# Masked attention with its mask, normalisation and projection steps in other slots, early key stores, and mixture layers computed in rows

## The chip, the cores and the metric

The kernel runs on one core of one Trainium2 chip. The metric is the device time of one execution in microseconds (us). The engines are named as the profile names them: PE (TensorE matmuls), PEld (its weight loads), DVE (VectorE), ACT (ScalarE), POOL (GpSimd) and SP (the sync engine, which here issues all loads and stores).

## The reference

A stack of four layer pairs works on x, 32 sequences of 56 tokens with 128 features, against a context of 32 x 1500 x 128. Every pair adds `tanh(g) * attention(layernorm(x), context)` and then `tanh(g) * ffn(layernorm(x))`. The change touches the first attention, and the third and the fourth feed-forward layer:

```python
# attention of pair 0: 16 heads of 8 features, with nan/inf clamps on q, k, v and the bias
logits = jnp.einsum('bhqd,bhkd->bhqk', q, k) * scale + bias
logits = jnp.where(mask == 0, -10000.0, logits)
probs = jax.nn.softmax(logits, axis=-1)
out = jnp.einsum('bhqk,bhkd->bhqd', probs, v)          # then @ W_o.T + b_o
# ffn of pair 2: 8 experts of one 128x128 matrix, top 2 of a softmax router, weights normalised
# ffn of pair 3: 8 experts with a bias each, top 1, weighted by its probability
out_all = jnp.einsum('th,ehd->ted', xt, expert_w) + expert_b[None, :, :]
e_out = jnp.take_along_axis(out_all, idx[:, None, None], axis=1)[:, 0, :]
y = gate[:, None] * e_out
```

## The kernel before

The program is a chain of blocks, and all engines meet between two of them: a block that loads x, then for each layer a `norm` block and the layer's own. In the trace the masked attention (`masked_attention`) covers about 0 to 1610 us, the other three attentions most of the rest; the two mixture layers in question lie at 4943 to 5027 us and 6161 to 6250 us.

**Masked attention.** It goes through the 32 sequences ("batches"). The 16 heads of a batch are handled in 8 pairs, one to a slot, p = 0 to 7; a pair has 2 x 56 = 112 query rows and 1500 keys. In slot p PE computes the pair's scores in two halves (`score(n, p, 0)` and `score(n, p, 1)`), transposes the logits of the pair of two slots ago in three portions (`turn`), and does one portion of other work. DVE turns each half's scores into logits with the bias and their maximum (`shifted(n, p, 0)` and `(n, p, 1)`), and `negate` closes the slot. There are two score buffers: `score(p, h)` waits until `shifted(p - 1, h)` is done. ACT subtracts the maximum, takes the exponential and copies PE's small results out.

Beside this, keys and values of batch n + 2 are prepared in batch n, in three portions each. PE computes the raw keys in slots 0 to 2 (`keys`) and the raw values in slots 3 to 5 (`values`); ACT copies keys out, DVE values (`keep_values`, slots 3 to 5). POOL guards each portion (`guard`: it clamps, 3 instructions), DVE takes the cleaned portion (`take`, slots 2 to 7: keys in 2 to 4, values in 5 to 7) and marks what is finite (`finite`). Keys are split in three bf16 parts (DVE's first, then POOL's `split`), stored to a scratch in DRAM (`store_keys`) and read back in packed form (`load_keys`) when the ring of packed keys has room. There are two buffers of key parts, so `take` of portion 2 in slot 4 waits for the store of portion 0. POOL's order in a batch is guard 0, guard 1, split 0, guard 2, split 1, guard 3, split 2, `blocks` (the queries of the next batch), guard 4, guard 5.

The mask of batch n + 1 arrives in three portions through one small buffer (`load_mask`), and DVE turns each into bf16 (`mark`, slots 0, 2 and 4). A load waits for the mark before it. The transposed mask (`load_mask_t`, one tile of 125 x 672, marked by `mark_t` in slot 5) serves two products in slots 0 and 1 of the next batch (`weigh_masked`), and its load waits until they are done. The end of a batch falls into the next one: `add_masked` in slot 5, PE's `sums` in slot 6, DVE's `normalise` (4 instructions, the first is the reciprocal) in slot 6, PE's output projection `out` at the end of slot 7, and ACT's `finish` at the head of slot 0 after it. SP issues everything in one written order, and each issue can wait on a semaphore, which holds back all behind it.

**Mixture layers.** `route` computes router logits and, in a chain of small DVE instructions, the combine weights `ffn_cw` (16 tiles of 112 tokens x 8 experts). PE then spreads each expert's weights over 128 partitions, 128 small matmuls, whose results ACT and DVE copy out. `experts`, a block of its own, multiplies the transposed input by an expert's weights on DVE and adds 8 x 4 products of 448 columns in PSUM. The result is feature by token, so the next `norm` block transposes it back and adds it to x.

## Time and profile before

| | |
|---|---|
| runs | 6254.1, 6254.86, 6259.9 us; median 6254.86 us |
| profiled execution | 6263.05 us, of which the span of its instructions is 6261.3 us |
| busy in the span | PE 86%, PEld 62%, DVE 71%, ACT 51%, POOL 29% |
| mean granted clock of PE | 0.927 |
| masked attention, 250 to 1500 us | PE busy 1116.20, DVE 1050.01, POOL 850.76, ACT 815.09 us of 1250; clock 0.92 |

A granted clock of 1.00 is 2.4 GHz, 0.50 is 1.2 GHz. Times in the timeline count from the span's start. An instruction's length can overlap the start of the next on its engine by about 0.1 us. "x2" merges instructions of one kind.

### The profile page before, as it was taken

To read this page: it belongs to the slowest core of one execution; us is meant where nothing else is said; L and a number is where in the kernel's file an instruction comes from. 1 tells how busy PE (TensorE), PEld (TensorE's weight loads), DVE (VectorE), ACT (ScalarE), POOL (GpSimd) and SP (SyncE) were. 2 spreads that over 40 slices of the span, in tenths; PEclk is the share of its full clock that TensorE was granted. 3 is DMA by queue.
4 is the path that set the end of the run, shared out by engine and by line. 5 is a ranking of instruction groups with operands and counts; after the bars stand their busy time and mean duration, and the time that the engine had idled before them with its cause. 6 is when DMAs were issued, how large, how long until landed. Compare 5 with 4: busy or idle time off the path is not lost. (4 is left out here: it accounts for less than half of the span.)

```text
span 6261.3 us, 134129 instructions
## 1 busy us (share of the span) xinstructions
PE 5379.5 (86%) x51967; PEld 3896.8 (62%) x51967; DVE 4432.3 (71%) x9168; ACT 3198.4 (51%) x5984; POOL 1820.4 (29%) x1426
## 2 busy tenths in 40 slices
PE   2888889899569999989749999999999759999997
PEld 1777777777258888877724444444444437888786
DVE  6888888887257777763458777777777437777774
ACT  0666666666236666652224444444444216666662
POOL 4767676763022222211101111111111012222220
PEclk6899999999679999989969999999999769999998
DMA  4555555553167777742010000000000048888880
GB/s 110 120 125 122 124 123 121 124 119 82 37 123 139 139 140 139 140 87 103 26 33 15 15 15 15 18 17 15 15 15 5 7 94 159 159 161 160 158 151 10
DMA packets 368548, 545.59 MB, mean 87 GB/s; under 512 B 115780, under 2 KB 248006, under 8 KB 367606
## 3 DMA queue, kind: packets, MB, share of 16 engines
q1 hardware_dynamic: 365894, 533.81, 41.7%
q8 instruction: 384, 6.29, 0.5%
q0 software_dynamic: 2048, 3.67, 0.2%
q14 instruction: 222, 1.82, 0.1%
HBM read 413.45 MB, written 123.90 MB: 86 GB/s over the span
## 5 line engine op out<-in xcount | busy, mean ns | idle before, releaser
L652 DVE CUSTOM_DVE_ANT_0 attn_logits<-attn_scores,attn_shift 112x750 f32<-112x750 f32 x1024 | 945.0, 933 | 441.3 <-PE attn_scores L456 441.3
L568 ACT ACTIVATE attn_probs_t<-attn_pt 125x448 f32<-125x448 f32 x1536 | 831.0, 542 | 579.3 <-PE attn_pt L471 559.0
L471 PEld LDWEIGHTS attn_pt<-ident,attn_logits 112*125 112x125 f32 x6144 | 850.9, 188 | 178.6 <-issue 92.5
L471 PE MATMUL attn_pt<-ident,attn_logits 112*125 112x112 f32 x6144 | 920.1, 273 | 25.5 <-ACT attn_logits L559 24.4
L2264 PE MATMUL attn2k_pk<-attn_wk,attn2k_cn_t 128*125 128x512 f32 x1536 | 738.7, 603 | 53.3 <-ACT attn2k_cn_t L2335 36.8
L2275 PE MATMUL attn2k_pg<-attn2k_kn,attn2k_cn 125*128 125x512 f32 x1536 | 725.0, 594 | 6.1 <-ACT attn2k_gram L2343 3.9
L2430 DVE TENSOR_REDUCE attn2k_ss<-attn2k_sq 125x16 f32<-125x1024 f32 x384 | 466.9, 1216 | 256.9 <-ACT attn2k_sq L2372 256.9
L385 POOL CAST attn_k_parts<-xn_t 128x500 bf16<-128x500 f32 x192 | 199.5, 1039 | 1421.6 <-DVE xn_t L622 1421.6
L1159 ACT ACTIVATE attn_probs_t<-attn_pt 125x448 f32<-125x448 f32 x768 | 414.9, 541 | 309.9 <-PE attn_pt L1047 308.2
L2372 ACT ACTIVATE attn2k_sq<-attn2k_pk 125x1024 f32<-125x1024 f32 x384 | 391.9, 1021 | 324.9 <-PE attn2k_pk L2264 324.8
L2264 PEld LDWEIGHTS attn2k_pk<-attn_wk,attn2k_cn_t 128*125 128x125 f32 x1536 | 273.1, 187 | 416.9 <-issue 321.0
L456 PE MATMUL attn_scores<-attn_k_packed,attn_q_blocks 96*112 96x375 bf16 x2048 | 514.4, 333 | 15.9 <-POOL attn_q_blocks L375 13.2
L1035 PE MATMUL attn_scores<-attn_k_packed,attn_q_blocks 96*112 96x375 bf16 x1024 | 357.4, 349 | 148.0 <-DVE attn_tops L1328 148.0
L2442 DVE TENSOR_TENSOR attn2k_kn<-attn2k_pk,attn2k_rn 125x1024 f32<-125x1024 f32 x384 | 470.0, 1224 | 13.3
L2275 PEld LDWEIGHTS attn2k_pg<-attn2k_kn,attn2k_cn 125*128 125x128 f32 x1536 | 264.1, 192 | 299.7 <-issue 287.9
L1328 DVE CUSTOM_DVE_ANT_0 attn_logits<-attn_scores,attn_bias,attn_floor 112x750 f32<-112x750 f32 x342 | 337.8, 988 | 101.6 <-PE attn_scores L1037 99.2
L1148 ACT ACTIVATE attn_logits<-attn_logits,attn_neg_top 112x750 f32<-112x750 f32 x342 | 313.0, 916 | 112.5 <-DVE attn_neg_top L1336 110.4
L559 ACT ACTIVATE attn_logits<-attn_logits,attn_neg_top 112x750 f32<-112x750 f32 x384 | 351.4, 915 | 4.1 <-DVE attn_neg_top L660 0.9
L2246 POOL COPY attn2k_q_now<-attn_q_t 128x448 f32 (+1 forms) x32 | 17.8, 557 | 1153.7 <-PE attn2k_pz L2296 1153.7
L412 PE MATMUL attn_side<-attn_ctx_t,attn_wk 128*128 128x500 f32 x384 | 221.5, 660 | 149.1 <-DVE xn_t L622 82.7
L484 PE MATMUL attn_po<-attn_probs_t,attn_v 125*32 125x112 f32 x12288 | 347.8, 261 | 1.5 <-ACT attn_probs_t L568 1.3
L1037 PE MATMUL attn_scores<-attn_masked,attn_pusher 112*112 112x375 bf16 x1024 | 344.8, 337 | 0.0
(364 smaller groups left out, 10562.6 us busy)
## 6 DMA issues: line engine op xcount, KB each, us to landing
attn_k_packed<-k_scratch SPq DMA_DIRECT2D x384, 375.0 KB, 6.4
attn_k_packed<-k_scratch SPq DMA_DIRECT2D x384, 187.5 KB, 3.9
k_scratch<-attn_k_parts SPq DMA_DIRECT2D x64, 1125.0 KB, 7.4
attn_ctx_t<-in_ctx_t SPq DMA_DIRECT2D x64, 750.0 KB, 7.3
k_scratch<-attn_k_parts SPq DMA_DIRECT2D x96, 375.0 KB, 4.4
attn_ctx_t<-in_ctx_t SPq DMA_DIRECT2D x96, 250.0 KB, 5.2
attn2k_ctx<-in_ctx SPq DMA_DIRECT2D x32, 750.0 KB
attn_mask_in<-in_mask SPq DMA_DIRECT2D x192, 109.4 KB
```

Source lines behind the costliest of these rows:

```text
L456: last = pe.matmul(scores[h][0:PAIR, b, 0:QTR], q_blocks[:, n % 2, p, :, :].rearrange("p a s -> p (a s)"), k_packed[:, n % 2, p, h * HALF ...
L471: last = pe.transpose(pt[(3 * at + t) % 2][0:KC, (c % 4) * PAIR:(c % 4 + 1) * PAIR], logits[:, at % 3, c * KC:(c + 1) * KC], g.ident[0:PAI ...
L559: act.activation(at, at, ACT.Identity, bias=neg_top[:, n % 2, p:p + 1]).then_inc(act_lowered, 1)
L568: act.activation(probs_t[0:KC, p // 4, 4 * t:4 * t + 4, (p % 4) * PAIR:(p % 4 + 1) * PAIR], pt[(3 * at + t) % 2][0:KC, 0:QUAD].rearrange(" ...
L652: dve.tensor_tensor_reduce(out=logits[:, at % 3, cols].rearrange("p (b k) -> p b k", b=2), in0=scores[h][0:PAIR, :, 0:QTR], in1=shift[:, n ...
L1035: pe.matmul(scores[h][0:PAIR, b, 0:QTR], q_blocks[:, n % 2, p, :, :].rearrange("p a s -> p (a s)"), k_packed[:, at % KEY_RING, cols], star ...
L1159: act.activation(probs_t[0:KC, at % PV_RING, 4 * t:4 * t + 4, :], pt[(3 * at + t) % 2][0:KC, 0:QUAD].rearrange("p (c q) -> p c q", c=4), A ...
L2264: last = pe.matmul(pk[c % 2][0:KC, b, :], cn_t[:, c % 2, :], wk[:, b * HW:(b + 1) * HW], start=True, stop=True)
L2275: last = pe.matmul(pg[:, b, :], cn[:, j, c, :], kn[:, c % 2, b * HW:(b + 1) * HW], start=(c == 0), stop=(c == CH - 1))
L2372: act.activation(sq[:, c % 2, :].rearrange("p (a b) -> p a b", a=2), pk[c % 2][0:KC, :, :], ACT.Square).then_inc(sq_ready, 1)
L2430: dve.tensor_reduce(ss[:, c % 2, :], sq[:, c % 2, :].rearrange("p (h d) -> p h d", h=H2), AX.X, ALU.add).then_inc(ss_ready, 1)
L2442: dve.tensor_tensor(kn[:, c % 2, :].rearrange("p (h d) -> p h d", h=H2), pk[c % 2][0:KC, :, :].rearrange("p a (h d) -> p (a h) d", h=8), r ...
```

## The change

It has four parts.

1. In the masked attention DVE's marks of the mask move: portions 1 and 2 of batch n + 1 to slots 1 and 2, portion 0 of batch n + 2 to the end of slot 7, and `mark_t` to slot 0 of the batch after. `normalise` moves from slot 6 to the end of slot 7, and the projection `out` from the end of slot 7 to slot 0, between the two score halves; ACT's `finish` goes behind the first exponential of slot 0.
2. SP's order changes with it: `store_keys` of portions 0 and 1 come ahead of the loads of the second half of the packed keys, and the loads of mask portions 1 and 0 move.
3. `mixture` replaces `route` and `experts` for the two layers. For each tile of 112 tokens PE computes all 8 experts' outputs (2 matmuls of 512 columns). For 11 tiles DVE multiplies them by the combine weights and sums over experts, for 5 tiles ACT scales and POOL adds. The sum is added to x in the block itself, so no expert-wise spread, no separate block and no transposition back remain. Layer 3 adds its bias by transposed weights, quarter by quarter.
4. The `norm` blocks after these layers get no gate, and the last one issues only the store of x.

```diff
                 for n in range(B):
                     if n + 1 < B:
+                        load_mask(n + 1, 1)
                         load_keys(n + 1, 0, (0, 1))
-                        load_mask(n + 1, 1)
                         load_keys(n + 1, 0, (2, 3))
                     load_mask_t(n)
                     if n + 1 < B:
...
-                    for i in range(3):
-                        if n + 1 < B:
-                            load_keys(n + 1, 1, (2 * i, 2 * i + 1))
-                        if n + 2 < B:
-                            store_keys(n + 2, i)
-                        if n + 3 < B:
+                    if n + 2 < B:
+                        store_keys(n + 2, 0)
+                        load_mask(n + 2, 0)
+                        store_keys(n + 2, 1)
+                    if n + 1 < B:
+                        load_keys(n + 1, 1, (0, 1, 2))
+                    if n + 2 < B:
+                        store_keys(n + 2, 2)
+                    if n + 1 < B:
+                        load_keys(n + 1, 1, (3, 4, 5))
+                    if n + 3 < B:
+                        for i in range(3):
                             load_ctx(n + 3, i)
                     if n + 2 < B:
-                        load_mask(n + 2, 0)
                         load_queries(n + 2)
...
                         if some:
                             turn(*prior, 0)
+                        if p == 0 and n > 1:
+                            out(n - 2)
                         score(n, p, 1)
...
-                        if p == 7 and n > 0:
-                            out(n - 1)
+                out(B - 2)
...
-                        if p == 0 and n > 1:
-                            finish(n - 2)
                         for t in range(3):
                             if prior[0] >= 0:
                                 exp(*prior, t)
+                            if p == 0 and t == 0 and n > 1:
+                                finish(n - 2)
...
-                        if p in (0, 2, 4) and n + 1 < B:
-                            mark(n + 1, p // 2)
-                        if p == 5:
-                            mark_t(n)
+                        if n + 1 < B and (p in (1, 2) or p == n == 0):
+                            mark(n + 1, p)
+                        if p == 0 and n > 0:
+                            mark_t(n - 1)
                         shifted(n, p, 1)
...
-                        if p == 6 and n > 0:
-                            normalise(n - 1)
                         if p == 7 and n + 1 < B:
                             floors(n + 1)
                         negate(n, p)
+                        if p == 7 and n + 2 < B:
+                            mark(n + 2, 0)
+                        if p == 7 and n > 0:
+                            normalise(n - 1)
+                mark_t(B - 1)
```

The core of the new `mixture`, behind a router chain that is the one of before (the output of an expert has 128 columns, `py` is a ring of 3 tiles of 2 PSUM banks):

```python
ACT_TILES = tuple(t for t in range(TILES) if t % 3 == 2)
DVE_TILES = tuple(t for t in range(TILES) if t % 3 != 2)
# PE, after the router's matmuls
for t in range(TILES):
    if t >= 3:
        if t - 3 in ACT_TILES:
            pe.wait_ge(parts_ready, ACT_TILES.index(t - 3) + 1)
        else:
            pe.wait_ge(scaled_ready, DVE_TILES.index(t - 3) + 1)
    for c in range(2):
        last = pe.matmul(py[t % 3][0:PAIR, c, :], g.xn_t[:, t * PAIR:(t + 1) * PAIR],
                         we[:, 4 * c:4 * c + 4, :].rearrange("p e d -> p (e d)"), start=True, stop=True)
    last.then_inc(y_ready, 1)
if b_experts is not None:
    for q in range(NQ):
        wait(pe, x_steps, 2 * q)
...
# DVE, once cw is there
for i, t in enumerate(DVE_TILES):
    dve.wait_ge(y_ready, t + 1)
    wait(dve, summed, i - 1)
    dve.tensor_tensor(scaled[:, i % 2, :, :], values(t),
                      cw[:, t, :].unsqueeze(2).broadcast_to((PAIR, E, D)), ALU.mult).then_inc(scaled_ready, 1)
    dve.wait_ge(scaled_ready, i + 1)
    dve.tensor_reduce(total[:, t, :], scaled[:, i % 2, :, :].rearrange("p e d -> p d e"), AX.X,
                      ALU.add).then_inc(summed, 1)
```

The order of the instructions shows what stands where. On SP, in the middle of a batch, this stood before, from the transposed mask's load on (`out_t` is the transposed mask, `mask_in` a mask portion, `k_parts` to `k_scratch` a key store, `k_packed` a load of packed keys):

```order
L821 DMA attn0_out_t<-in_mask0_t 125x672
L817 DMA attn0_mask_in<-in_mask0 56x500 x2
L843 DMA attn0_k_packed<-k_scratch 16x4x1500 x2
L880 DMA y_scratch<-y_t 128x56
L843 DMA attn0_k_packed<-k_scratch 16x4x1500 x2
L832 DMA k_scratch<-attn0_k_parts 128x3x500
L812 DMA attn0_ctx_t<-in_ctx_t 128x500
```

and this stands there now:

```order
L822 DMA attn0_out_t<-in_mask0_t 125x672
L818 DMA attn0_mask_in<-in_mask0 56x500 x2
L844 DMA attn0_k_packed<-k_scratch 16x4x1500 x2
L881 DMA y_scratch<-y_t 128x56
L833 DMA k_scratch<-attn0_k_parts 128x3x500
L818 DMA attn0_mask_in<-in_mask0 56x500 x2
L833 DMA k_scratch<-attn0_k_parts 128x3x500
```

The first store of keys no longer stands behind a load of packed keys. The mask portion right behind the transposed mask is portion 2 in both, but its mark now stands in slot 2 and no longer in slot 4.

On DVE, at the end of slot 7 and in slot 0 (L1328 and L1335 are `shifted`, the row that writes only `tops` belongs to it), before:

```order
L1328 ISA x_sb,attn0_tops<-attn0_scores1,attn0_bias,attn0_floor 112x750
L1328 ISA attn0_tops 112x1
L1316 TENSOR_SCALAR attn0_floor<-attn0_counted 112x1
L1318 TENSOR_SCALAR attn0_floor<-attn0_floor 112x1
L1336 TENSOR_SCALAR attn0_neg_top<-attn0_tops 112x1
L1328 ISA attn0_logits0,attn0_tops<-attn0_scores0,attn0_bias,attn0_floor 112x750
L1328 ISA attn0_tops 112x1
L1258 TENSOR_SCALAR attn0_masked<-attn0_mask_in 112x500
```

and now:

```order
L1335 ISA x_sb,attn0_tops<-attn0_scores1,attn0_bias,attn0_floor 112x750
L1335 ISA attn0_tops 112x1
L1323 TENSOR_SCALAR attn0_floor<-attn0_counted 112x1
L1325 TENSOR_SCALAR attn0_floor<-attn0_floor 112x1
L1343 TENSOR_SCALAR attn0_neg_top<-attn0_tops 112x1
L1265 TENSOR_SCALAR attn0_masked<-attn0_mask_in 112x500
L1363 RECIPROCAL xn_t<-attn0_side 128x224
L1365 TENSOR_TENSOR xn_t<-attn0_mixed,xn_t 128x224
L1367 TENSOR_TENSOR attn0_mixed<-xn_t 128x224
L1369 COPY_PREDICATED xn_t<-attn0_mixed,attn0_zero 128x224
L1335 ISA attn0_logits0,attn0_tops<-attn0_scores0,attn0_bias,attn0_floor 112x750
```

A mark and the four instructions of `normalise` now stand between the end of slot 7 and the first logits of slot 0.

On PE, from the last product of slot 7 to the second score half of slot 0 (L1020 and L1026 are the projection), before:

```order
L1060 MATMUL attn0_po<-attn0_probs_t,attn0_v 32x112 x24
L1020 MATMUL attn0_side<-xn_t,attn0_wo 128x56 x4
L1035 MATMUL attn0_scores0<-attn0_k_packed,attn0_q_blocks 112x375
L1037 MATMUL attn0_scores0<-attn0_masked,attn0_pusher 112x375
L1035 MATMUL attn0_scores0<-attn0_k_packed,attn0_q_blocks 112x375
L1037 MATMUL attn0_scores0<-attn0_masked,attn0_pusher 112x375
L1047 MATMUL attn0_pt0<-ident,attn0_logits1 125x112 x4
L1035 MATMUL attn0_scores1<-attn0_k_packed,attn0_q_blocks 112x375
```

and now:

```order
L1066 MATMUL attn0_po<-attn0_probs_t,attn0_v 32x112 x24
L1041 MATMUL attn0_scores0<-attn0_k_packed,attn0_q_blocks 112x375
L1043 MATMUL attn0_scores0<-attn0_masked,attn0_pusher 112x375
L1041 MATMUL attn0_scores0<-attn0_k_packed,attn0_q_blocks 112x375
L1043 MATMUL attn0_scores0<-attn0_masked,attn0_pusher 112x375
L1053 MATMUL attn0_pt0<-ident,attn0_logits1 125x112 x4
L1026 MATMUL attn0_side<-xn_t,attn0_wo 128x56 x4
L1041 MATMUL attn0_scores1<-attn0_k_packed,attn0_q_blocks 112x375
```

The projection, which waits for `normalise`, stands ahead of the second score half of slot 0.

## Rows read from the trace of the kernel before

**Rows 1.** Waits, 250 to 1500 us: total us, times, longest us.

```profile
DVE attn_k_parts L1286 <- DMA k_scratch<-attn_k_parts: 46.8, 28, 2.1
```

**Rows 2.** Timeline of PE: start us, length us, instruction, [idle before].

```profile
807.25 0.56 PE L1035 MATMUL attn_scores<-attn_k_packed,attn_q_blocks 96*112 96x375 bf16 x1 [4.12 <-DVE attn_tops L1328]
...
812.83 0.37 PE L1035 MATMUL attn_scores<-attn_k_packed,attn_q_blocks 96*112 96x375 bf16 x1
...
818.33 0.32 PE L1035 MATMUL attn_scores<-attn_k_packed,attn_q_blocks 96*112 96x375 bf16 x1
...
821.22 1.10 PE L1020 MATMUL attn_side<-xn_t,attn_wo 128*128 128x56 f32 x8
...
823.22 0.32 PE L1035 MATMUL attn_scores<-attn_k_packed,attn_q_blocks 96*112 96x375 bf16 x1
...
831.85 0.37 PE L1035 MATMUL attn_scores<-attn_k_packed,attn_q_blocks 96*112 96x375 bf16 x1
...
851.46 0.56 PE L1035 MATMUL attn_scores<-attn_k_packed,attn_q_blocks 96*112 96x375 bf16 x1 [3.84 <-DVE attn_tops L1328]
```

**Rows 3.** Timeline of DVE, the same stretch.

```profile
836.71 0.82 DVE L1258 TENSOR_SCALAR attn_masked<-attn_mask_in 112x500 bf16<-112x500 int32 x1
...
843.83 0.68 DVE L1296 TENSOR_TENSOR y_t<-attn_side,attn_bv 125x512 f32<-125x512 f32 x1
...
861.36 1.54 DVE L1356 RECIPROCAL xn_t<-attn_side 128x224 f32<-128x224 f32 x1
...
864.15 0.20 DVE L1336 TENSOR_SCALAR attn_neg_top<-attn_tops 112x1 f32<-112x1 f32 x1
...
865.19 0.78 DVE L1303 COPY_PREDICATED attn_v<-attn_good,y_t 125x512 f32<-125x512 int32 x1
...
867.29 1.00 DVE L1328 CUSTOM_DVE_ANT_0 x_sb<-attn_scores,attn_bias,attn_floor 112x750 f32<-112x750 f32 x1
```

**Rows 4.** Timeline of POOL, the same stretch.

```profile
844.67 0.62 POOL L934 TENSOR_SCALAR y_t<-y_t 125x512 f32<-125x512 f32 x1
...
849.49 0.73 POOL L944 CAST attn_k_parts<-attn_clean_late 128x500 bf16<-128x500 f32 x1 [1.06 <-DVE attn_clean_late L1288]
...
860.33 1.25 POOL L937 TENSOR_TENSOR attn_v<-attn_v,y_t 125x512 f32<-125x512 f32 x1
```

**Rows 5.** Timeline of SP, its DMA issues, the same stretch.

```profile
831.98 0.28 SPq L821 DMA_DIRECT2D attn_out_t<-in_mask_t  x1
837.56 0.76 SPq L817 DMA_DIRECT2D attn_mask_in<-in_mask  x2
```

**Rows 6.** Windows; last three columns: clock, DMA share, GB per s.

```profile
834.00:837.80 3.80, 3.80 (x64) 2.96 (x63) 3.73 (x6) 2.82 (x5) 2.58 (x4) 1.00 0.20 80
839.70:841.00 1.30, 1.30 (x13) 1.21 (x12) 1.23 (x3) 1.19 (x2) 1.30 (x1) 1.00 1.10 180
```

**Rows 7.** Timeline, all engines, the two mixture layers.

```profile
4961.23 0.29 DVE L1680 TENSOR_TENSOR ffn_cw<-route_hot 112x128 f32<-112x128 f32 x1
...
5032.64 3.18 DVE L197 BATCH_NORM_STATS2 norm_stats<-x_sb 112x6 f32<-112x128 f32 x16
...
6174.96 0.29 DVE L1659 TENSOR_TENSOR ffn_cw<-route_hot,route_m 112x128 f32<-112x128 f32 x1
...
6207.65 0.53 ACT L1627 ACTIVATE ffn_cw_t<-route_pb 8x448 f32<-8x448 f32 x1 [0.73 <-PE route_pb L1611]
...
6251.91 3.12 DVE L183 SCALAR_TENSOR_TENSOR x_sb<-last_py,gates,x_sb 112x512 f32<-112x512 f32 x4 [8.00 <-PE last_py L158]
6255.06 0.34 SPq L230 DMA_DIRECT2D out<-x_sb  x1
```

**Rows 8.** The page's costliest groups: xcount, busy us, mean ns, idle us.

```profile
L2264 PE MATMUL attn2k_pk<-attn_wk,attn2k_cn_t 128*125 128x512 f32 x1536 | 738.7, 603 | 53.3 <-ACT attn2k_cn_t L2335 36.8
...
L2430 DVE TENSOR_REDUCE attn2k_ss<-attn2k_sq 125x16 f32<-125x1024 f32 x384 | 466.9, 1216 | 256.9 <-ACT attn2k_sq L2372 256.9
...
L2442 DVE TENSOR_TENSOR attn2k_kn<-attn2k_pk,attn2k_rn 125x1024 f32<-125x1024 f32 x384 | 470.0, 1224 | 13.3
```

More of the change, by code:

```diff
@@ L1613, in _ @@
                         last.then_inc(turned, 1)
+                        pe.wait_ge(cw_t_ready, q + 1)
+                        for t in range(4 * q, 4 * q + 4):
+                            last = pe.matmul(pb[0:PAIR, (t % 4) * D:(t % 4 + 1) * D], cw_t[:, t * PAIR:(t + 1) * PAIR],
+                                             be[:], start=True, stop=True)
+                        last.then_inc(bias_ready, 1)
             @block.scalar
@@ L1618, in _ @@
                 act.activation(p[:], p[:], ACT.Exp).then_inc(exp_ready, 1)
-                for i in range(0, E * NQ, 2):
-                    e, q = divmod(i, NQ)
-                    act.wait_ge(spread, i + 1)
-                    act.activation(cwb[:, e, q * QUAD:(q + 1) * QUAD], pb[i % 4][:, 0:QUAD],
-                                   ACT.Copy).then_inc(act_used, 1)
-                if cw_t is not None:
+                act.wait_ge(cw_ready, 1)
+                for i, t in enumerate(ACT_TILES):
+                    act.wait_ge(y_ready, t + 1)
+                    wait(act, halved, i - 1)
+                    for e in range(E):
+                        last = act.activation(parts[:, i % 2, e, :], values(t)[:, e, :], ACT.Copy, scale=cw[:, t, e:e + 1])
+                    last.then_inc(parts_ready, 1)
+                if b_experts is not None:
                     for q in range(NQ):
                         act.wait_ge(turned, q + 1)
-                        act.activation(cw_t[:, q * QUAD:(q + 1) * QUAD], pb[q][0:E, 0:QUAD],
-                                       ACT.Copy).then_inc(act_used, 1)
+                        act.activation(cw_t[:, q * QUAD:(q + 1) * QUAD], pb[0:E, 0:QUAD], ACT.Copy).then_inc(cw_t_ready, 1)
+            @block.gpsimd
+            def _(pool):
+                for i, t in enumerate(ACT_TILES):
+                    at = i % 2
+                    pool.wait_ge(parts_ready, i + 1)
+                    pool.tensor_tensor(halves[:, at, :, :], parts[:, at, 0:4, :], parts[:, at, 4:8, :], ALU.add).then_inc(halved, 1)
+                    pool.wait_ge(halved, i + 1)
+                    pool.tensor_tensor(halves[:, at, 0:2, :], halves[:, at, 0:2, :], halves[:, at, 2:4, :],
+                                       ALU.add).then_inc(added, 1)
+                    pool.wait_ge(added, 2 * i + 1)
+                    pool.tensor_tensor(total[:, t, :], halves[:, at, 0, :], halves[:, at, 1, :], ALU.add).then_inc(added, 1)
             @block.vector
@@ L1730, in ffn2 @@
[L1730 to L1745 removed]
+                dve.wait_ge(cw_ready, 1)
@@ new lines, in _ @@
+                dve.wait_ge(summed, len(DVE_TILES))
+                for q in range(NQ):
+                    rows = g.x[:, 4 * q:4 * q + 4, :].rearrange("p t d -> p (t d)")
+                    dve.wait_ge(added, 2 * sum(t < 4 * q + 4 for t in ACT_TILES))
+                    if b_experts is not None:
+                        dve.wait_ge(bias_ready, q + 1)
+                        dve.scalar_tensor_tensor(rows, pb[0:PAIR, :], g.gates[:, gate:gate + 1], rows,
+                                                 ALU.mult, ALU.add).then_inc(x_steps, 1)
+                        dve.wait_ge(x_steps, 2 * q + 1)
+                    dve.scalar_tensor_tensor(rows, total[:, 4 * q:4 * q + 4, :].rearrange("p t d -> p (t d)"),
+                                             g.gates[:, gate:gate + 1], rows, ALU.mult, ALU.add).then_inc(x_steps, 1)
@@ L2606, in program @@
                 mask=a["mask3"]), "add"),
-            lambda: ffn3(nc, g, a),
+            lambda: mixture(nc, g, "ffn3", a, a["router3"], a["router3_b"], "top1", a["experts3"], 7, a["experts3_b"]),
         ]
```

143 lines of the change are left out of this document (44 added, 99 removed).

## The prediction, made before the changed kernel ran

> **What bounds the kernel now.** I read the timeline of one batch of the masked attention first, engine by engine, because the change touches every one of the 30 batches that still prepare keys (n = 0 to 29), then the chain of waits for how often a wait recurs, then the timeline of the mixture layers. One batch takes 44.2 us: the second score half of slot 5 starts at 807.25 and, a batch later, at 851.46 [rows 2]. It is the only place where PE waits long, 4.12 and 3.84 us, and it waits for DVE's logits of slot 4. DVE itself had stood for the DMA that stores key portion 0; such waits sum to 46.8 us in 28 batches, 1.7 us each [rows 1]. After the wait PE runs at half clock: the score matmul at 807.25 takes 0.56 us, the same one at 823.22 0.32 us [rows 2].
>
> So the batch is a ring. From the wait on PE works without a pause to slot 2 (812.83 is the head of slot 6, 823.22 the second score half of slot 0, 831.85 the head of slot 2), and from there DVE, loaded with `take`, sets the pace to the end of slot 4. The slow stretch is on it: slot 5's work took 5.6 us (807.25 to 812.83); in the other slots such work runs at twice the speed, and I put the loss at 2.3 us.
>
> **The mixture layers.** Removed is all from `ffn_cw` to x. In layer 2 that is 4961.52 to 5032.64 (the first instruction of the next norm on x), 71.1 us; in layer 3 6175.25 to 6255.06, 79.8 us [rows 7]. What replaces it goes by DVE. An eight-expert tile is 1024 elements wide; a product and a reduction of that width cost 1.224 and 1.216 us [rows 8], with handover 2.5 us, and 11 tiles 27.5 us. PE needs at most 0.96 us per matmul of 512 columns (738.7 us over 768 of them, two records each) [rows 8], so 1.9 us per tile, 5.8 per three tiles against DVE's 5.0 for its two of three. But it is three tiles ahead when the weights arrive, and those rows include a slow clock and waits; I take 28.5 us in layer 2, where it has idled before, 27.5 in layer 3. ACT's and POOL's five tiles lie beside. Then four additions, 3.12 us [rows 7], and 1.1 us to the next block: 32.7 us, a saving of 38.4. In layer 3 the bias makes each quarter a chain of transposes, a copy of 0.53 us [rows 7], products and two additions of 0.78 each; the first hides behind DVE's tiles. I put the first at 1.6 and the other three at 4.0 each (below 2.1, the copy and additions alone; above 6): 27.5 + 1.6 + 12 + 1.1 = 42.2, a saving of 37.6. Together 76 us. The bound on the poor side is the reduction: its input here is strided, no row shows that, and at half rate 11 x 1.2 x 2 = 27 us would be lost. I take no loss, since the product and the reduction, which read in different patterns, cost the same.
>
> **The masked attention: what goes.** The key store no longer stands behind a load of packed keys that waits for slot 4, and is issued as POOL's first split ends, some 5 us earlier; the 1.7 us go. So does one mark of 0.8 us from slot 4 [rows 3], the transposed mask's from slot 5, and `normalise`, 861.36 to 864.15, 2.8 us [rows 3], from slot 6. DVE then reaches the value portions sooner. What is late next is POOL.
>
> **What binds then.** POOL is continuous from guard 3 at 844.67 to the end of guard 5 at 861.58, save 1.06 us of waiting for DVE [rows 4]: 15.85 us of work, none of it changed. Guard 3 begins when DVE has copied value portion 0 (843.83 + 0.68 = 844.51 [rows 3]), and DVE's slot 7 cannot go past `take` of portion 2 before guard 5 ends. Before, that `take` stood at 865.19, 3.6 us later than needed. DVE's own work between these two points falls from 20.7 us (844.44 to 865.19) to 20.7 - 1.6 - 0.8 - 0.4 - 2.8 = 15.1, so POOL is the later one by about 0.8 us.
>
> Behind that `take`: 865.19 to 867.29, 2.1 us, led to the logits of slot 0 [rows 3]; now a mark (0.4 us where POOL rests, by half of the 0.82 beside it) and `normalise` stand there too: 5.3 us. PE's projection waits for it, and the second score half of slot 0 stands behind the projection: 0.1 + 0.9 us. From there to slot 2 is unchanged, 823.22 to 831.85, 8.6 us [rows 2]. PE idles ahead of the projection. From slot 7's second score half to that point PE has 823.22 - 818.33 - 0.9 = 4.0 us of work [rows 2], DVE from the same instant at least 0.9 + 0.9 + 0.5 + 0.4 + 2.8 = 5.5 us, and POOL's delay adds to it: 2 to 3 us of idling, in slots where nothing hides it.
>
> **A new wait in slot 2.** Mask portion 2 is now marked in slot 2, due at 836.71 [rows 3]. Its load stands on SP behind the transposed mask, which waits until slot 1's masked products end: issued at 831.98 [rows 5], its 328 KB go at 80 GB/s and a low DMA share until 837.8 [rows 6]. Before, the portion was issued at 837.56, for slot 4, and nobody waited. Now it is issued at once, but moves behind the big load: 219 KB at the 180 GB/s of the next window [rows 6] are 1.2 us, to 839.0. If the portion uses other DMA engines it is there at 835.6 and there is no wait. I take 838.6, a wait of 1.9 us (bounds 0 and 2.3).
>
> The Trainium skill, page "DMA: Bandwidth & Descriptors", section "Why a DMA increments its semaphore by 16 and not by 1", says that a load from SP runs on the largest number of engines up to 16 that divides its outer dimension, the lowest-numbered ones: 5 for this mask of 125 rows, 14 for a portion of 56 rows, which share those 5; and descriptors of an engine are taken in ring order ("Queues, rings and completion order"). The DMA share of 0.20 agrees roughly (5 of 16 would be 0.31). By the rule the wait is there in every batch; without it, 29 x 1.9 = 55 us would fall out of the sum.
>
> **The sum of a batch.** From the head of slot 2: 844.51 - 831.85 = 12.7; mask wait 1.9; POOL 0.15 + 15.85 + 0.1; DVE 5.3; projection 1.0; PE to slot 2 8.6. That is 45.6 us, against 44.2. The old 2.3 us of slow clock are no longer on the ring, but three waits of 2 to 3 us (slots 3, 5, 0) replace the one of 4. Whether a wait of that length lowers the clock no row shows, since PE's next longest wait in a batch of before is far shorter than 3.84. So the cost lies between 0 and 2.3 us; I take 0.7, nearer to nothing, since the waits are shorter and only the part that falls in slots 0 and 1 counts. The batch becomes 46.3, +2.1 us, in 29 periods +61 us. Prologue and tail change by less than 2 us.
>
> In all 6263 - 76 + 61 = 6248 us for the profiled execution. The median is 8.2 us below that execution, so I predict **6240 us**.
>
> **Rivals.**
> (a) The forecast: mask wait, POOL's chain, a little slow clock. 6240, own range 6215 to 6270. Chance 0.42.
> (b) Slower: the wait ahead of the projection lowers the clock for as long as the old one did. The place is slots 0 and 1, the price 2.3 us on the ring, so 47.9 us a batch: 6255 - 76 + 107 = 6286. It decides against the change once the clock costs over 1.6 us a batch. For it: the length of the wait, 2 to 3 us of PE doing nothing, each batch. Against it: 4 us were needed in the only row. 0.15. The skill's page "TensorE: Matmul & The Clock Gate" ("HAM oscillation") tells of a kernel where a short wait before each group of matmuls starts every group at half clock; by that rule (b) is the likely one.
> (c) The mask portion is not late. 43.7 us plus 0.7 of clock, +0.2 a batch: 6185, range 6165 to 6200. For it: the DMA engines are mostly idle in that window. 0.22.
> (d) The moves in the attention change nothing, DVE and PE rearranging the same 44.2 us: 6179. 0.08.
> (e) POOL runs faster beside a less loaded DVE, and DVE's 15.1 us and no mask wait give 42.9 us a batch: 6141. 0.08.
> (f) (a) with the strided reduction at half rate: 6267. 0.05.
>
> A difference of 0.2% (12.5 us) is about what can be told from none, so faster means below 6242. Half of (a), and (c), (d), (e): 0.58; same, most of the rest of (a) and half of (f): 0.23; slower: 0.19. The range leaves out (e) and most of (b): 6165 to 6285.
>
> **What would show it.** In the changed profile: DVE no longer waits for the DMA of `k_scratch`; it waits about 1.9 us for `attn_mask_in` before the mark in slot 2, some 29 times; `take` in slot 7 waits for POOL by about 1 us; PE waits 2 to 3 us for `normalise` ahead of the projection; a batch repeats every 46 us. The tail from `ffn_cw` is 33 us in layer 2 and 42 in layer 3. The prediction is wrong if the mask portion lands before it is due (then c), if the clock falls to half through slots 0 and 1 (then b), or if a tile's reduction takes over 2 us (then f).

## The result and the profile after

The changed kernel takes 6408.14 us (median of 4 runs, 6403.79 to 6431.82), the kernel before beside it 6257.38 us. The ratio is 1.0249, 95% interval 1.0222 to 1.0276: **2.5% slower**, where 6240 us and a small gain were forecast. The profiled execution is the longest of the four, 6431.82 us with a span of 6429.7; the others lie 20 to 28 us below it.

The starts of PE's transposes in the `norm` blocks part the span into layers. The two profiled executions:

| part | before | after | difference |
|---|---|---|---|
| masked attention and the norm before it | 14.1 to 1592.3 | 14.3 to 1807.1 | +214.5 |
| first feed-forward layer (untouched) | 95.3 | 110.2 | +14.9 |
| layers between (untouched) | 3249.5 | 3249.2 | -0.3 |
| layer 2, mixture | 101.2 | 67.9 | -33.3 |
| last attention (untouched) | 1117.2 | 1116.7 | -0.5 |
| layer 3, mixture, to the end | 105.9 | 78.8 | -27.1 |

The untouched first feed-forward layer took 92.2 to 110.2 us from one profiled kernel of this study to the next; it ran part of that time at the low clock (the 20 us from 1847 have a granted clock of 0.50). It is no effect of the change: in e5 below, which holds the whole change, the layer takes 92.4 us.

**The attention.** From one projection to the next a batch takes 51.2 us (mean of 28 periods, 50.3 to 52.0), before 44.4. The view of waits between 250 and 1500 us, as in [rows 1]:

```profile
DVE attn_logits L1335 <- PE attn_scores L1043: 155.8, 66, 4.8
...
PE attn_scores L1041 <- DVE attn_tops L1335: 127.4, 72, 4.4
...
DVE attn_masked L1265 <- DMA attn_mask_in<-in_mask: 84.0, 24, 4.2
...
PE attn_side L1026 <- DVE xn_t L1369: 80.5, 25, 3.5
...
DVE attn_v L1310 <- POOLq L945: 25.3, 24, 1.1
```

DVE's wait for `k_scratch` is gone. In its place stand DVE's wait for the mask in slot 2 (84.0 / 24 = 3.5 us each), PE's wait for `normalise` ahead of the projection (80.5 / 25 = 3.2 us) and DVE's for POOL in slot 7 (25.3 / 24 = 1.05 us). PE's timeline of one batch, to be laid beside [rows 2]:

```profile
816.20 1.96 PE L1026 MATMUL attn_side<-xn_t,attn_wo 128*128 128x56 f32 x8 [3.20 <-DVE xn_t L1369]
817.95 0.52 PE L1041 MATMUL attn_scores<-attn_k_packed,attn_q_blocks 96*112 96x375 bf16 x1
...
820.01 1.90 PE L997 MATMUL attn_side<-attn_ctx_t,attn_wk 128*128 128x500 f32 x2
...
823.94 0.37 PE L1041 MATMUL attn_scores<-attn_k_packed,attn_q_blocks 96*112 96x375 bf16 x1
...
828.82 0.37 PE L1041 MATMUL attn_scores<-attn_k_packed,attn_q_blocks 96*112 96x375 bf16 x1
...
838.25 0.37 PE L1041 MATMUL attn_scores<-attn_k_packed,attn_q_blocks 96*112 96x375 bf16 x1 [3.32 <-DVE attn_tops L1335]
...
839.36 1.71 PE L1003 MATMUL attn_side<-attn_wv,attn_ctx_t 128*125 128x128 f32 x8
...
866.51 1.63 PE L1026 MATMUL attn_side<-xn_t,attn_wo 128*128 128x56 f32 x8 [3.21 <-DVE xn_t L1369]
867.93 0.52 PE L1041 MATMUL attn_scores<-attn_k_packed,attn_q_blocks 96*112 96x375 bf16 x1
```

The projection takes 1.96 us behind its wait (1.10 before), the score matmul 0.52 (0.32 before), the two key products of slot 0 1.90. At 823.94, the head of slot 1, the clock is back. From the projection to the head of slot 2 at 828.82 it is 12.6 us. In each of the 28 batches the granted clock falls to 0.50 at this wait, and the projection takes more than 1.10 us. The second wait of the batch, 3.32 us in slot 3, comes from the mask: DVE waits for it, so its logits are late, and PE waits for them. The clock falls behind this wait too, in all 28 batches, but in 16 of them only for about half as long, and the score matmul directly behind it is slow in 12. From 250 to 1500 us the granted clock is 0.89 (0.92 before). DVE in the same batch, beside [rows 3]:

```profile
810.95 0.80 DVE L1310 COPY_PREDICATED attn_v<-attn_good,y_t 125x512 f32<-125x512 int32 x1 [1.06 <-POOLq L945]
...
812.91 0.41 DVE L1265 TENSOR_SCALAR attn_masked<-attn_mask_in 112x500 bf16<-112x500 int32 x1
813.24 1.55 DVE L1363 RECIPROCAL xn_t<-attn_side 128x224 f32<-128x224 f32 x1
...
815.68 0.46 DVE L1369 COPY_PREDICATED_SCALAR xn_t<-attn_mixed,attn_zero 128x224 f32 x1
...
836.86 0.42 DVE L1265 TENSOR_SCALAR attn_masked<-attn_mask_in 112x500 bf16<-112x500 int32 x1 [2.92 <-DMA attn_mask_in<-in_mask]
```

SP's queue, beside [rows 5]:

```profile
828.95 0.28 SPq L822 DMA_DIRECT2D attn_out_t<-in_mask_t  x1
829.27 1.57 SPq L818 DMA_DIRECT2D attn_mask_in<-in_mask  x2
830.88 0.84 SPq L844 DMA_DIRECT2D attn_k_packed<-k_scratch  x2
831.77 0.42 SPq L881 DMA_DIRECT2D y_scratch<-y_t  x1
```

The mask portion is issued 0.3 us behind the transposed mask and marked 7.6 us after its issue. The windows of those microseconds (length, busy times of PE, PEld, DVE, ACT and POOL with their counts, granted clock, DMA share, GB/s), beside [rows 6]:

```profile
830.00:831.00 1.00, 1.00 (x10) 0.91 (x8) 1.00 (x3) 0.81 (x2) 1.00 (x1) 1.00 0.46 90
...
832.00:833.00 1.00, 1.00 (x33) 0.89 (x35) 0.97 (x2) 1.00 (x2) 0.61 (x1) 1.00 0.94 298
833.00:834.00 1.00, 1.00 (x34) 0.80 (x24) 0.94 (x2) 0.78 (x2) 0.32 (x1) 1.00 1.11 118
834.00:835.00 1.00, 0.93 (x8) 0.70 (x5) 0.00 (x0) 0.00 (x0) 0.92 (x2) 1.00 0.88 117
```

From 832 to 835 the DMA engines are full (0.94, 1.11 and 0.88; a transfer counts in the window in which it starts, so a share can exceed 1), with two loads of packed keys of 188 KB behind the masks.

**The mixture layers**, beside [rows 7, 8]:

```profile
5190.76 0.29 DVE L1711 TENSOR_TENSOR ffn_cw<-ffn_hot 112x128 f32<-112x128 f32 x1
5191.09 1.22 DVE L1716 TENSOR_TENSOR ffn_scaled<-ffn_py,ffn_cw 112x1024 f32<-112x1024 f32 x1
5192.35 1.92 DVE L1719 TENSOR_REDUCE ffn_total<-ffn_scaled 112x128 f32<-112x1024 f32 x1
...
5225.09 2.74 DVE L1730 SCALAR_TENSOR_TENSOR x_sb<-ffn_total,gates,x_sb 112x512 f32<-112x512 f32 x4
5228.66 3.19 DVE L197 BATCH_NORM_STATS2 norm_stats<-x_sb 112x6 f32<-112x128 f32 x16 [0.83 <-PEq L105]
...
6370.93 0.29 DVE L1693 TENSOR_TENSOR ffn_cw<-ffn_hot,ffn_m 112x128 f32<-112x128 f32 x1
...
6405.32 0.75 DVE L1727 SCALAR_TENSOR_TENSOR x_sb<-ffn_pb,gates,x_sb 112x512 f32<-112x512 f32 x1
6406.11 0.75 DVE L1730 SCALAR_TENSOR_TENSOR x_sb<-ffn_total,gates,x_sb 112x512 f32<-112x512 f32 x1
6410.60 0.75 DVE L1727 SCALAR_TENSOR_TENSOR x_sb<-ffn_pb,gates,x_sb 112x512 f32<-112x512 f32 x1 [3.74 <-PE ffn_pb L1638]
```

The sum over experts (L1719) takes 1.92 us, the product (L1716) 1.22, so 11 tiles last 34.0 us in both layers (5191.09 to 5225.09). Behind them the last three quarters of layer 3 come every 5.28 us (6405.32, 6410.60), of which DVE stands 3.74.

### The profile page after: what moved, and what is told of

Read it like the earlier page. It is cut to its first block and busy times, and to the rows that moved or that the text cites. A ratio compares the mean times of both kernels' runs of the same rounds, so it can differ in the third digit from the quotient of the medians.

```text
span 6429.7 us, 133121 instructions
## 1 busy us (share of the span) xinstructions
PE 5433.5 (85%) x51447; PEld 3900.8 (61%) x51447; DVE 4426.2 (69%) x9168; ACT 3197.0 (50%) x6024; POOL 1862.6 (29%) x1456
## 5 line engine op out<-in xcount | busy, mean ns | idle before, releaser
L472 PEld LDWEIGHTS attn_pt<-ident,attn_logits 112*125 112x125 f32 x6144 | 853.0, 189 | 179.8 <-issue 94.6
L1335 DVE CUSTOM_DVE_ANT_0 attn_logits<-attn_scores,attn_bias,attn_floor 112x750 f32<-112x750 f32 x342 | 338.5, 990 | 201.4 <-PE attn_scores L1043 201.0
L1053 PEld LDWEIGHTS attn_pt<-ident,attn_logits 112*125 112x125 f32 x2052 | 320.8, 209 | 53.6 <-issue 27.4
```

Of the source, the lines that this page charges most:

```text
L472: last = pe.transpose(pt[(3 * at + t) % 2][0:KC, (c % 4) * PAIR:(c % 4 + 1) * PAIR], logits[:, at % 3, c * KC:(c + 1) * KC], g.ident[0:PAI ...
```

## Experiments

Each kernel ran beside the kernel before on the same chip; what counts is the ratio, since the kernel before itself took 6288 us on the chip of the first four and 6256 to 6259 us later. In the four profiles from that chip the untouched second feed-forward layer takes 390 us, in the others 358 to 359, which is nearly the whole difference; it is in both kernels of a ratio. A period is the mean of the same 28 batches. All keep the changed mixture layers.

### One part alone, and one part undone

**e1** is the kernel before with parts 3 and 4 of the change only.

> The kernel before with the two mixture layers alone changed. The stage lengths of the changed kernel (layer 2: 101.2 to 67.9 us, last layer to the end: 105.9 to 78.8 us) say -60 us, so about 6197 us. The prediction's terms (-38.4 and -37.6) said -76, so 6181. If the layers cost something elsewhere (the slow stretch of the first hidden layer, 95.3 to 110.2 us, seen in the changed kernel) it is 6212.

Measured: ratio 0.9915 (0.9899 to 0.9932), 6234.68 against 6288.2 us, -53.5; period 44.4 us. Layer 2 takes 67.9 us here too. So the mixture layers give 54 to 60 us, not 76, and the loss is all in the attention. Its period is that of the kernel before.

**e2** changes the order of two loads of the changed kernel:

```diff
-                    load_mask_t(n)
                     if n + 1 < B:
                         load_mask(n + 1, 2)
+                    load_mask_t(n)
+                    if n + 1 < B:
                         load_keys(n + 1, 0, (4, 5))
```

> The changed kernel, with the third mask portion's load issued ahead of the transposed mask's load. Theory (two waits per batch, each with a slow clock behind it): the 3.5 us wait of DVE for the mask in slot 2 goes, with PE's 3.3 us wait in slot 3 and some 1.5 us of slow clock behind it: -4.8 x 29 = -139, about 6269 us. Rival one (the transfer is slow by itself, not for what is ahead of it): only the issue 2.2 us earlier counts, -64, 6344. Rival two (the mask wait lies in the shadow of another limit of the ring): above 6390.

Measured: 1.0046 (1.003 to 1.0063), period 46.8, -4.4 us. The theory's time, a little less. DVE does not wait for the mask at all. This run also has projections with the low clock and without it. Two projections of it, one batch apart:

```profile
807.84 1.96 PE L1027 MATMUL attn_side<-xn_t,attn_wo 128*128 128x56 f32 x8 [3.21 <-DVE xn_t L1370]
809.60 0.52 PE L1042 MATMUL attn_scores<-attn_k_packed,attn_q_blocks 96*112 96x375 bf16 x1
...
855.85 1.10 PE L1027 MATMUL attn_side<-xn_t,attn_wo 128*128 128x56 f32 x8 [1.78 <-DVE xn_t L1370]
856.78 0.33 PE L1042 MATMUL attn_scores<-attn_k_packed,attn_q_blocks 96*112 96x375 bf16 x1
```

Behind a wait of 3.2 us PE is at half clock (score matmul 0.52 us), behind one of 1.78 us it is not (0.33). The 20 batches that begin in the first way take 47.2 to 48.3 us, the eight of the second way (waits of 1.76 to 2.05 us) 44.6. That splits the 4.4 us. The 20 batches take 47.7 us in the mean, 3.5 below 51.2, which is the mask wait and nothing more; the other 0.9 is the eight batches in which the projection's low clock stays away, 3.1 us each. So the 1.5 us of slow clock that the theory put behind the mask wait does not appear in the time.

**e3** undoes the other wait: `normalise` back in slot 6, `out` at the end of slot 7, ACT's `finish` back ahead of the first exponential of slot 0 (not in the cut below), and the masks as changed.

```diff
+                        if p == 6 and n > 0:
+                            normalise(n - 1)
                         negate(n, p)
                         if p == 7 and n + 2 < B:
                             mark(n + 2, 0)
-                        if p == 7 and n > 0:
-                            normalise(n - 1)
...
-                        if p == 0 and n > 1:
-                            out(n - 2)
...
+                        if p == 7 and n > 0:
+                            out(n - 1)
```

> The changed kernel, with the normalisation back in slot 6 and the output projection back at the end of slot 7; the masks stay where the change put them. Theory (two waits per batch): PE's 3.2 us wait ahead of the projection goes, and the 2.3 us that slots 0 and 1 lose at the low clock: -5.5 x 29 = -160, about 6249 us. Rival (the wait only moves: DVE's normalisation in slot 6 makes PE wait there instead, as the 4 us wait of the kernel before): -1.5 x 29, about 6365.

Measured: 1.0051 (1.0034 to 1.0068), period 46.9, -4.3 us. The mask wait stays (100.2 us in 27 times, 3.7 each). PE waits elsewhere (143.7 us for DVE's logits), so the rival has a share, but most of the loss goes.

**e4** has both edits.

> The changed kernel with both edits: third mask portion's load ahead of the transposed mask's, normalisation in slot 6, projection at the end of slot 7. Theory with the two waits independent: 51.2 - 4.8 - 5.5 = 40.9 us per batch, about 6109 us. Rival (another limit, the chain through POOL's guards, or one wait per batch that stays as in the kernel before): 42.7 us per batch (44.4 less the 1.7 us wait for the key stores), about 6161.

Measured: 0.9845 (0.9829 to 0.9861), 6190.02 us, period 42.8: -8.4 us a batch, the sum of 4.4 and 4.3 less 0.3. The two edits nearly add up, and without the two waits the rest of the change is a gain. The theory's 40.9 was too low, since each edit was worth 4.3 and not 4.8 or 5.5; the period of 42.8 is the rival's 42.7.

### What each wait is made of

**e5** leaves the changed kernel's waits as they are and keeps PE busy in front of the projection:

```diff
                         if p == 0 and n > 1:
+                            pe.wait_ge(logits_ready, 2 * n * HP)
+                            for i in range(18):
+                                pe.matmul(scores[1][0:PAIR, i % 2, 0:QTR],
+                                          q_blocks[:, n % 2, p, :, :].rearrange("p a s -> p (a s)"),
+                                          k_packed[:, (n * HP) % KEY_RING, 0:QTR], start=True, stop=True)
                             out(n - 2)
```

> The changed kernel with 18 useless score matmuls in front of the projection in slot 0, in the place where PE idles 3.2 us; their result is overwritten, and nobody waits for more than before. This prices the clock alone. Theory (the wait makes slots 0 and 1 run at half clock): from projection to the head of slot 2 9.6 us instead of 12.6, -3.0 x 29 = -87 us, ratio to the kernel before 1.0249 - 0.0139 = 1.011. Rival (slots 0 and 1 are long for another reason, such as DVE or ACT): no gain, ratio 1.025 or more.

Measured: 1.0107 (1.0084 to 1.013), period 48.0, -3.2 us. One batch:

```profile
821.34 3.03 PE L1105 MATMUL attn_scores<-attn_k_packed,attn_q_blocks 96*112 96x375 bf16 x18
824.71 1.10 PE L1026 MATMUL attn_side<-xn_t,attn_wo 128*128 128x56 f32 x8 [0.34 <-DVE xn_t L1374]
825.65 0.33 PE L1041 MATMUL attn_scores<-attn_k_packed,attn_q_blocks 96*112 96x375 bf16 x1
...
826.72 1.02 PE L997 MATMUL attn_side<-attn_ctx_t,attn_wk 128*128 128x500 f32 x2
...
834.28 0.37 PE L1041 MATMUL attn_scores<-attn_k_packed,attn_q_blocks 96*112 96x375 bf16 x1
```

18 matmuls of no use fill 3.03 us, the projection takes 1.10 us, and the head of slot 2 comes 9.6 us behind it (834.28 - 824.71), against 12.6. DVE's instructions and their order are the same, and the semaphore wait added is the one that the second score half makes anyway, a little later. So of the 4.3 us that e3 gives back, 3.2 are PE's clock, 3.0 of them between the projection and slot 2, and by difference 1.1 the late `normalise` itself. This prices the clock nearly alone (behind the mask wait too the slow stretch is the long one in 7 batches instead of 12); it is the largest term that the prediction missed.

**e6** loads only 5 of the 125 rows of the transposed mask from batch 1 on, in the changed kernel's order; the output lacks the rest of it.

> The changed kernel, its queue order and waits untouched, but from batch 1 on only 5 of the 125 rows of the transposed mask are loaded (the rest of that input to the output is left out). The load of mask portion 2 is issued no earlier, about 0.5 us behind the head of slot 2, but almost nothing is ahead of it. Theory A (the portion is late for the bytes ahead of it): no wait of DVE for it, -4.3 us a batch as when it was issued ahead, ratio 1.005. Theory B (it is late for its own issue, 2 us too late): DVE still waits 1 to 2 us, ratio about 1.015. Both give less than 1.0249.

Measured: 1.004 (1.0026 to 1.0054), period 46.8, as in e2. SP's queue in one batch, and DVE's mark in slot 2 of the same:

```profile
821.82 0.28 SPq L823 DMA_DIRECT2D attn_out_t<-in_mask_t  x1
822.14 0.76 SPq L818 DMA_DIRECT2D attn_mask_in<-in_mask  x2
```

```profile
826.53 0.82 DVE L1266 TENSOR_SCALAR attn_masked<-attn_mask_in 112x500 bf16<-112x500 int32 x1
```

The portion is issued no earlier in the batch than before the edit (0.3 us behind the transposed one, 0.45 us behind the head of slot 2, in both), and 4.4 us later it is marked without a wait, against 7.6. Theory A: it was late for the bytes of the transposed mask ahead of it. The packed keys behind it are still there, so they alone do not make it late.

**e7** is e2 with the projection moved two steps down in slot 0, behind the second half's scores and transposes.

> The changed kernel with the third mask portion's load first and the projection two steps later in slot 0, behind the second score half and its transposes; the normalisation stays in slot 7. Theory (PE waits only since it is asked for the projection while DVE normalises): the 3.2 us wait shrinks to about 1.5, the clock stays high, 42.8 us a batch as with the normalisation in slot 6, ratio 0.985. Rival (the rest of the wait is enough to lower the clock, or the second half stands behind DVE anyway): only the 1.7 us of work moved into the wait, ratio 0.997.

Measured: 0.9982 (0.997 to 0.9994), period 46.2: the rival.

```profile
842.31 1.10 PE L1027 MATMUL attn_side<-xn_t,attn_wo 128*128 128x56 f32 x8 [1.59 <-DVE xn_t L1370]
844.01 2.01 PE L998 MATMUL attn_side<-attn_ctx_t,attn_wk 128*128 128x500 f32 x2 [0.60 <-ACT y_t L1190]
```

PE's timeline again: the wait is 1.59 us and not 3.2, but 0.60 us more follows, and the key products take 2.01 us (1.02 at full clock). In 20 of 28 batches the key products take about 2 us, and those batches 45.8 to 47.5 us; in the other eight they take 1.08, and the batch 44.3. A wait of half the length does not protect: here the clock fell at waits of 1.52 to 2.15 us in most batches, in e2 behind 1.76 to 2.05 us in none.

**e10** combines e2 and the useless matmuls of e5.

> The changed kernel with the third mask portion's load first and the 18 useless matmuls in PE's wait ahead of the projection in slot 0. Theory (with no mask wait and no low clock in slots 0 and 1, what is left is the 3.2 us in which PE stands for DVE's normalisation): 46.9 - 3.0 = 43.9 us a batch, ratio 0.991. Rival (the low clock then comes from the wait in slot 5, 2.3 us, as in a third of the batches of that kernel, 44.6): ratio 0.994.

Measured: 0.9937 (0.9922 to 0.9953), period 44.8: the rival's number. PE stays at full clock in slots 0 and 1, and the granted clock falls in slot 5 in all 28 batches: in 25 for about half the time that it stays low behind a 3.2 us wait, and these take 44.4 to 44.8 us; in three for the whole of it, so that it reaches slot 6, and these take 46.0 to 46.2. No batch is without it, so whether the low clock of slot 5 is the rival's reason is not shown by this run. Against e4's 42.8 the late `normalise`, without the low clock in slots 0 and 1, costs 2 us a batch, not 1.1: the 1.1 was measured with the mask wait in the same batch.

**e11** is e4 with 12 useless matmuls in slot 5, ahead of the 2.28 us in which PE waits for DVE there.

> The changed kernel with the third mask portion first, normalisation in slot 6, projection at the end of slot 7, and 12 useless matmuls (2 us) in slot 5, where PE waits 2.3 us for DVE and then runs at half clock through slot 5. Theory (DVE has no pause there and is the limit, so the clock of PE costs nothing on that stretch): no change, ratio 0.984 to 0.985. Rival (the slow slot 5 is on the path): up to -2.3 us a batch, ratio 0.974.

Measured: 0.9858 (0.9843 to 0.9873), period 42.8 as in e4. The granted clock never falls in these 28 batches (1.00 from 250 to 1430 us, 0.97 in e4), and nothing is gained: DVE is the limit on that stretch. There was less to gain than the rival's 2.3, though. In e4 the clock falls in 18 of 28 batches, in 15 of them for about 3.4 us and in three for 6.8, half of which is 1.3 us a batch (an estimate from these stretches). The low clock costs 3.2 us where PE's work is the ring (slots 0 and 1) and none of its 1.3 here.

### The rest of the change

**e9** is the kernel before with the mixture layers and the new order of SP; marks, `normalise` and `out` are back in their old slots.

> The kernel before with the mixture layers in rows and the new queue order (early key stores) alone: masks, normalisation and projection in their old slots. Theory (the early store is the whole gain of 1.6 us a batch that the kernel with both waits undone has left; moving marks out of slot 4 brings nothing): 42.8 us a batch, ratio 0.985. Rival (the mark in slot 4 matters, since DVE is busy without pause from slot 2 to slot 5): 43.6, ratio 0.988; if the store does nothing by itself, 44.4 and 0.9915.

Measured: 0.9862 (0.9847 to 0.9877), period 43.4. The new order of SP, with DVE's wait for the store gone, gives 1.0 of e4's 1.6 us a batch. The rest would be the moved marks', but 0.9862 and 0.9845 are not told apart by their intervals.

**e8** is e4 with the product of the mixture layers written with the expert innermost, so that the sum reads consecutive elements.

```diff
-dve.tensor_tensor(scaled[:, i % 2, :, :], values(t),
+dve.tensor_tensor(scaled[:, i % 2, :].rearrange("p (d e) -> p e d", e=E), values(t),
...
-scaled[:, i % 2, :, :].rearrange("p e d -> p d e"), AX.X,
+scaled[:, i % 2, :].rearrange("p (d e) -> p d e", e=E), AX.X,
```

> The changed kernel with the third mask portion first, the normalisation in slot 6, the projection at the end of slot 7, and in the mixture layers the product written with the expert innermost, so that the sum over experts reads consecutive elements. Theory (the strided read makes the sum 1.92 us instead of 1.22): the sum falls to 1.2 us, -0.7 x 22 = -15 us, ratio 0.9845 - 0.0025 = 0.982. Rival (the strided write costs the product what the sum gains): ratio 0.9845, product about 1.9 us.

Measured: 0.9843 (0.9826 to 0.9859). The rival:

```profile
L1716 DVE TENSOR_TENSOR ffn_scaled<-ffn_py,ffn_cw x16: 1980/2000/2025, 4937.9 to 6130.6; 112x1024 f32<-112x1024 f32 x16
L1719 DVE TENSOR_REDUCE ffn_total<-ffn_scaled x15: 1219/1220/1221, 4939.9 to 6129.5; 112x128 f32<-112x1024 f32 x15
```

The sum falls to 1.22 us and the product rises from 1.22 to 2.00. Reading at a step of 512 bytes costs 0.7 us per 1024 elements, writing at a step of 32 bytes 0.8: the price only changes sides.

**e12** is e4 with six more PSUM banks for the bias of layer 3: the transposed weights and the bias of quarters 1 to 3 go to two banks each that the tiles no longer use, PE makes all four transposes ahead of the first bias product, and it no longer waits for DVE's additions.

> The same kernel without the useless matmuls; in the last mixture layer each quarter's transposed weights and bias have a PSUM bank of their own, so PE does not wait for DVE's additions. Theory (the 5.3 us a quarter are the single bank's chain): the last three quarters take 1.6 us each, -11 us, ratio 0.9845 - 0.0018 = 0.983, the kernel's best. Rival (PE's own transposes and products, 3.0 us a quarter at half clock, set the pace): -6 us, ratio 0.9835.

Measured: 0.983 (0.9816 to 0.9843), 6149.35 us, the lowest ratio of the study, though its interval overlaps that of e4 (0.9829 to 0.9861).

```profile
6133.14 0.75 DVE L1733 SCALAR_TENSOR_TENSOR x_sb<-ffn_pb,gates,x_sb 112x512 f32<-112x512 f32 x1 [0.52 <-PE ffn_pb L1644]
...
6136.52 0.75 DVE L1733 SCALAR_TENSOR_TENSOR x_sb<-ffn_py,gates,x_sb 112x512 f32<-112x512 f32 x1 [0.17 <-PE ffn_py L1644]
...
6138.23 0.75 DVE L1733 SCALAR_TENSOR_TENSOR x_sb<-ffn_py,gates,x_sb 112x512 f32<-112x512 f32 x1 [0.17 <-PE ffn_py L1644]
```

A quarter now takes 1.7 us, and the last layer to the end 68.7 us instead of 78.8: 10 us less, where the theory had 11.

## Why the prediction was wrong

It failed in the step **"I take 0.7"** for the low clock, with bounds of 0 and 2.3 us. The clock falls behind the projection's wait, in each of 28 batches of the changed kernel, and costs 3.2 us a batch (e5): more than the upper bound. The bound was read off the old place, slot 5. The windows of the two slow stretches, first before, then after (length, busy times of PE, PEld, DVE, ACT and POOL, clock, DMA share, GB/s):

```profile
805.90:812.70 6.80, 5.45 (x36) 4.88 (x36) 6.80 (x13) 2.83 (x5) 6.64 (x6) 0.50 0.43 116
```

```profile
815.80:822.50 6.70, 6.30 (x22) 4.99 (x22) 2.91 (x8) 3.01 (x5) 0.00 (x0) 0.50 0.37 67
```

The stretch at the low clock is as long as before. But in slot 5 DVE is busy through all of it, so the time that PE loses there is most likely hidden, and the prediction was most likely wrong to put that stretch on the ring (e11 shows this for e4; no run tests it on the kernel before). In slots 0 and 1 DVE is busy for 2.91 of 6.70 us and PE is alone on the ring. PE also works for more of it, 6.30 us against 5.45, and half of 6.30, the time that full clock would save, is 3.15 us: the 3.2 that e5 measured. No batch of the kernel before had a row for such a wait, but its trace had one, at the last projection of the same layer:

```profile
1570.09 1.69 PE L1020 MATMUL attn_side<-xn_t,attn_wo 128*128 128x56 f32 x8 [3.00 <-DVE xn_t L1362]
```

It waits 3.00 us for the same `normalise` and takes 1.69 us instead of 1.10, with the clock falling to 0.50 from 1570.4 us on. PE had stood for part of the time before it too, but the row spoke for rival (b). The Trainium skill, page "TensorE: Matmul & The Clock Gate", section "HAM oscillation — how this bites in real kernels", has it that a kernel with a wait before each group of matmuls starts every group cold; the changed kernel does so in each batch. By the argument "4 us were needed in the only row" I gave that case 0.15.

The profiled execution lies 184 us above the 6248 that were forecast for it: 153 in the attention (214.5 against 61), 16 in the mixture layers, 15 in the untouched first feed-forward layer. The period was to be 46.3 us and is 51.2. Of these 4.9 us the clock has 2.5 (3.2 against 0.7), the mask wait 1.6 (3.5 against 1.9) and POOL's chain 2.0, and 1.3 went the other way; the last two are read from one batch.

Point by point, for the batch from the head of slot 2 at 828.82 to the next at 879.32 (50.5 us, forecast 46.3):

- Slot 2 to the first copied value portion: 14.6 us forecast (12.7 and the mask wait of 1.9), 14.3 measured (843.13). The wait alone was mis-sized: 3.5 us in the mean, above the bound of 2.3, while DVE's other work took less. The step that failed is "219 KB at the 180 GB/s of the next window are 1.2 us": the window it was read from had no transposed mask in flight, and here the portion follows it onto full DMA engines (0.94, 1.11 and 0.88 from 832 to 835); with only 5 rows of the transposed mask it is in time (e6). The wait costs 3.5 us of the period (e2).
- POOL from there to `take` of the last portion: 16.1 us forecast, 18.1 measured (to 861.26). The direction was right, `take` waits 1.05 us, but I counted POOL's work only; it stood 0.6 us for DVE's rest of key portion 2 and began 0.8 us after the copy, not 0.15. The remaining 0.8 us are its own instructions (16.66 us against 15.85), which the forecast took as unchanged.
- `take`, mark and `normalise` to the projection: 5.3 forecast, 5.25 measured (861.26 to 866.51). PE's wait was to be 2 to 3 us and is 3.2.
- The projection to the head of slot 2: 1.0 + 8.6 forecast, with 0.7 for the clock 10.3; 12.8 measured.
- The wait for the key stores (1.7 us) goes, as forecast; e9 measures 1.0 for it.
- Outside the ring's periods the attention loses another 24 us: 214.5 - 28 x 6.8. The first batch is 9 us later (253.06 against 244.14), the one after the 28 takes 44.5 instead of 32.7. "Prologue and tail change by less than 2 us" was wrong.
- The mixture layers: -76 forecast, -60.4 measured. The step is "I take no loss" for the strided sum: 1.92 us, not 1.22, so 34.0 us for 11 tiles where 28.5 and 27.5 were set, 12 us in both layers. The argument was two rows of another layer that cost the same; they said nothing of this layout. The Trainium skill has the figure, on the page "Vector Engine (DVE) Microarchitecture Reference", section "5.2 Measured stream behaviour on trn2": about 1.7 ns per column where one port hops at every element (by 4 KiB there, by 512 bytes here) against 1.05 without; for 1024 columns that is an estimate of 1.8 us. The trace agrees roughly: 1.92 us, and 1.22 without the step (e8). The bias quarters took 5.28 us where 4.0 was set, since PE's part ran at the low clock (0.91 and 2.04 us, in the first quarter 0.55 and 1.12) and had to wait for both additions first (e12); the four additions were right (2.74 for 3.12).

What was right: which waits go, which come and where, and that the mixture layers gain. Of the rivals (b) named the mechanism, with a price of 2.3 instead of 3.2 and a mask wait of 1.9 instead of 3.5; 6286 us was its time, still 122 us below the measured one. (c), (d) and (e) are refuted, (f) had the place and twice the price. The range did not allow for the clock, the mask and the sum over experts all being worse than set.

## What to carry to other kernels

Price a new wait of the matmul engine with the slow stretch behind it. In the 28 batches of each of these kernels every wait of 3.2 us or more lowered the clock, and waits of 1.5 to 3.05 us did so in some batches and not in others. Then ask where that stretch lies: it cost 3.2 us where the engine is on the ring and nothing that could be measured where another engine is. Look for the new wait in the whole trace of the old kernel, its tail too, and not only in one period. A few useless matmuls in the wait measure this price and can stay in as a repair. A load that was harmless becomes late when its data are due earlier and it goes out right behind a larger one: then its time is that of the bytes ahead of it, not its own (7.6 us from issue to use, at most 4.4 with most of those bytes left out). And a vector instruction that steps at every element, reading or writing, took 1.6 times the plain one.

## What was not expected of the hardware

- The clock behind waits of the same length differs. PE's wait of about 2.28 us in slot 5 lowered it in 8 of 28 batches of e2, 18 of e4, 26 of e7 and 28 of e10. At the projection, 1.76 to 2.05 us in e2 never lowered it, and 1.52 to 2.15 us in e7 did in 20 of 28. In e2, e7 and e10 fast and slow batches also come in a repeating order. The wait's length alone does not decide; what else does is left open.
- The untouched first feed-forward layer varies by 18 us between kernels, with a granted clock of 0.50 or 1.00 in it. It may be part of the 20 to 28 us by which the profiled execution lies above the others, which have no trace.
